# Window mixing with group normalization: group means ahead of the products, variances behind them, statistics ahead of the additions

## The chip, the cores and the metric

The kernel runs on one core of one Trainium2 chip, in float32. The metric is the device time of one execution in microseconds (us), lower is better. The engines are TensorE (PE, matrix products; PEld is its loading of weights), VectorE (DVE), ScalarE (ACT), GpSimd (POOL) and the queue that starts most transfers (SP). The change touches the first stage, the mixing of windows, and one link of the second, the projections.

## The reference

The input is x of 8 images, 256 channels, 64 by 64 pixels. Two blocks follow each other, each behind a group normalization (32 groups of 8 channels, over channels and pixels):

```
m = mean(g); s = var(g); (g - m) / sqrt(s + eps)          # per image and group
x = x + mix(gn(x), w, b)      # windows of 8x8 pixels, shifted by 4: 16 heads, each a 64x64 product over
                              # the pixels of a window, for its 16 channels, plus a bias
x = x + attention(gn(x), ...) # 1x1 projections to q, k, v, a 5x5 depthwise and a grouped 1x1 convolution,
                              # linear attention with relu, projection, batch norm
```

## The kernel before

**Stages.** `window_mixing` computes the first line and writes its result to `x1_dram`. `projections`, `convolved_heads` and `output` compute the second. A stage begins when the one before has ended on all engines. This case is about `window_mixing`, with eight images `b` in two halves `g` of rows: 16 steps `s`, even for g = 0 and odd for g = 1. The 256 channels lie on 128 partitions in two tiles (`ct`).

**One step.** The half image is normalized into `xn` (ScalarE and GpSimd, `normal_slots`), transposed by TensorE so that pixels lie on partitions (`turn`, four groups of 8 transposes, line 534), copied to `xT` by ScalarE (`fill`, line 460), multiplied with the weights (`mix`, line 559), given its bias and copied to `yT` (`add_bias`: two of eight parts by VectorE, line 683, six by ScalarE, line 468), transposed back (`turn_back`, four blocks of 8 transposes, line 571) and added to the image in place (`add_back`, VectorE, lines 698 and 702). SP then stores the half image and, when that has landed, loads the same half of the image three further on into the place.

**The order on TensorE** is written out by hand. In step s: the products of s, in four quads of heads; `turn(s + 1, 0)`, `turn(s + 1, 1)`, `turn_back(s, 0)`, `turn(s + 1, 2)`, `turn_back(s, 1)`, `turn(s + 1, 3)`, `turn_back(s, 2)`, `turn_back(s, 3)`. There are eight banks of PSUM: quad k writes banks 2k and 2k + 1, groups 0 and 2 of `turn` banks 2 and 3, groups 1 and 3 banks 0 and 1, blocks 0 and 2 of `turn_back` banks 4 and 5, blocks 1 and 3 banks 6 and 7. So block 2 waits for the addition of block 0 (`k_taken`), block 3 for that of block 1, and quad 2, the third, for all four additions of the step before. Block 0 waits for all the biases.

**The normalization of the next image** needs statistics. VectorE takes them from the image in SBUF in eight pieces a step (`moments(b + 2, g)`, line 111: `bn_stats` over 512 pixels), two images ahead. In each even step s = (b, 0) a chain for image b + 1 runs through three engines (`norm_scale`, `norm_group_sums`, `norm_std`):

- aggregate: VectorE gathers the pieces (`moments` in `norm_scale`, line 120), two instructions;
- `means`: TensorE averages the means over a group (line 161), into `stat_ps`;
- `centre`: VectorE copies the mean (127) and adds its squared distance to the variance (128 to 130), which are chained by a semaphore;
- `variances`: TensorE averages these (line 165);
- `variance`: VectorE adds eps (line 134), and increments `var`;
- root: ScalarE (line 171), behind the second `fill` of the next step;
- `scale`: VectorE makes scale and shift in six chained instructions (138 to 148); ScalarE and GpSimd wait for these with the normalization of step s + 2.

`chain_at(b, g)` says which steps have a chain: the even ones of images 0 to 6, and the last step, 15, whose chain (tiles `p_...`) is for the first image that the projections take. Both sums lie in bank 0 (`stat_ps = ps[:, 0, 0:4]`), which quad 0 fills, so TensorE takes the means behind the products and behind VectorE's bias of quad 0, the variances behind `turn(s + 1, 0)`, and `turn(s + 1, 1)`, which writes bank 0 again, waits for `var`.

**The order on VectorE** in a step: aggregate (chain step), two biases, `centre`, two pieces, `variance`, one piece, `scale`, and then four additions with a piece behind each, and the last piece. In steps without a chain it is the same without the links. Steps 12 and 14 and their odd neighbours have fewer images ahead: step 12 has no pieces; in 13 and 14 the pieces are those of the projections' first image; step 15 has none.

All engines execute their instructions in the order written, and wait for semaphores where the code says so.

Of the kernel before, what the change touches and what calls it, by code (L numbers as in the profile page):

```python
# [25 lines left out]
ALU = mybir.AluOpType  # L26
# [88 lines left out]
def norm_scale(dve, chain, b, T, mv, bst, stat_ps, sem, mean=None, normal_done=None):  # L115
# [16 lines left out]
    def variance():  # L132
        dve.wait_ge(sem["group_sum"], 2 * b + 2)
        dve.tensor_scalar(T["ve"][:, :], stat_ps[:, 2:4], GN_EPS, None, ALU.add).then_inc(sem["var"], 1)
# [22 lines left out]
def norm_group_sums(pe, b, T, mv, stat_ps, gavg, sem):  # L157

    def means():
        pe.wait_ge(sem["moments"], 2 * b + 1)  # L160
        pe.matmul(stat_ps[:, 0:2], gavg[:, :], mv[:, :, 0], start=True, stop=True).then_inc(sem["group_sum"], 1)

    def variances():
        pe.wait_ge(sem["moments"], 2 * b + 2)
        pe.matmul(stat_ps[:, 2:4], gavg[:, :], T["vc"][:, :], start=True, stop=True).then_inc(sem["group_sum"], 1)
    return means, variances
# [14 lines left out]
def make_constants(nc, ctx, two_phases, K):  # L181

    def sb(name, shape, dt=F32):
        return ctx.enter_context(nc.sbuf_tensor(name, shape, dt))
# [19 lines left out]
    K["p_mv"] = sb("pmv", [P, CT, 2])  # L204
    K["p_norm"] = norm_tiles(sb, lambda name: ctx.enter_context(nc.semaphore(name)), "p")
# [45 lines left out]
def window_mixing(nc, K, x_in, w_mix, b_mix, w_qkv, w_dw, x1_dram, taps_dram):  # L251
# [3 lines left out]
    with ExitStack() as ctx:  # L255
# [30 lines left out]
        def norm_of(b):  # L286

            return (0, K["p_norm"][0], K["p_mv"], K["p_norm"][1], None) if b == B else (b, T, mv, ns, mean)

        ps = psum("mix_ps", [P, 8, 512])  # L290
        stat_ps = ps[:, 0, 0:4]
# [206 lines left out]
        def _(pe):  # L498
            halves = (slice(0, WS * WS), slice(WS * WS, P))

            def links(b):
                image, Tn, mvn, nsn, _ = norm_of(b)
                return norm_group_sums(pe, image, Tn, mvn, stat_ps, K["gavg"], nsn)
# [35 lines left out]
            def mix(s):  # L539

                b, g = STEPS[s]
                pe.wait_ge(t_taken, N_T * (s + 1))
                for k in range(QUADS):
                    if k == 2:
                        at_least(pe, k_taken, N_K * s)
# [33 lines left out]
            for s, (b, g) in enumerate(STEPS):  # L579
                mix(s)  # L580
# [3 lines left out]
                if means:  # L584
                    pe.wait_ge(m_taken, len(BY_DVE) * s + 1)
                    means()
                if more:
                    turn(s + 1, 0)
                if variances:
                    variances()  # L590
                if more:
                    if image is not None:
                        pe.wait_ge(ns["var"], image + 1)
                    turn(s + 1, 1)
# [10 lines left out]
        def _(dve):  # L605
# [20 lines left out]
            def chain_of(b):  # L626
                image, Tn, mvn, nsn, mean_n = norm_of(b)

                def normal_done():
                    if 0 < b < B:  # L630
# [3 lines left out]
                                                            mean_n, normal_done)  # L634
# [36 lines left out]
            for g in range(GROUPS):  # L671
                for _ in moments(1, g):
                    pass
            dve.wait_ge(b_ready, 1)
# [30 lines left out]
            for s, (b, g) in enumerate(STEPS):  # L705
# [8 lines left out]
                if image is not None:  # L714
                    begin, centre, variance, scale = chain_of(image)
                    begin()
# [3 lines left out]
                if image is not None:  # L720
                    centre()
                for _ in range(2):
                    next(pieces, None)
                if image is not None:
                    variance()
                next(pieces, None)
                if image is not None:
                    scale()
                for n in range(BACKS):
                    add_back(s, n)  # L730
                    next(pieces, None)
                for _ in pieces:
                    pass
# [3 lines left out]
def projections(nc, K, x1_dram, qkv_dram, qr_dram, w_pw, bn_in, taps_dram, sorted_dram):  # L737
# [3 lines left out]
    with ExitStack() as ctx:  # L741
# [451 lines left out]
        def _(dve):  # L1193
# [64 lines left out]
            def body(i, last_body):  # L1258
                for par in range(2):
# [3 lines left out]
                    gather, centre, variance, scale = norm_scale(dve, Chain(dve, ns["chain"]), b + 1, T, mv, bst, stat_ps, ns)  # L1263
# [960 lines left out]
```

## Time and profile before

| | |
|---|---|
| median of 3 runs | 2491.38 us (2490.16 to 2492.57) |
| profiled execution | 2490.49 us, its span 2488.8 us |
| mixing stage in the profile | from 0 to 261 us |
| TensorE busy over the span | 2364.8 us, 95% |
| mean granted TensorE clock | 0.984 of full speed |

In the rows further down, a line of the timeline says when a run of like instructions started, how long it lasted, the engine, the line of the kernel and the operation, output <- input, with their number, and in brackets how long the engine idled before it and who released it. Two lines of the same engine can overlap a little, since the next instruction starts while the last one writes its end. The ends of matmuls are modelled.

### The profile page before, as it was taken

Reading aid. Unit: us, or ns where it says so; the run is one execution under the profiler, and the core shown is the slowest. Engines: PE = TensorE matmul, PEld = TensorE weight load, DVE = VectorE, ACT = ScalarE, POOL = GpSimd, SP = SyncE. Lnnn points to the kernel's source line nnn. Section 1 sums busy time; section 2 is a strip of 40 time slices with the busy share of each in tenths; the row PEclk is TensorE's granted clock in tenths of the full one; section 3 lists DMA queues with packets and bytes.
Section 4 is the critical chain, followed back from the end, with each engine's and each line's share of the span. In section 5 each row is a group of like instructions: output and inputs, shape, how many; then the busy total and the mean of one; then the engine's idle time right before and its main releaser. Section 6 shows DMA issues by size and latency. Waiting matters only on the chain. (4 is left out here: it accounts for less than half of the span.)

```text
span 2488.8 us, 66780 instructions
## 1 busy us (share of the span) xinstructions
PE 2364.8 (95%) x25485; PEld 1886.2 (76%) x25485; DVE 1992.4 (80%) x2652; ACT 1495.8 (60%) x1864; POOL 1099.0 (44%) x1477
## 2 busy tenths in 40 slices
PE   5999799999999999799999999999999889999998
PEld 5889687777787788577888888888888656666666
DVE  7887588787688786788888888888888578888775
ACT  5777576665566566566677677667767433443342
POOL 6722387787787787300000000000000068888887
PEclk9999899999999999899999999999999999999999
DMA  7874688988889889988888888888888677777774
GB/s 283 342 293 177 212 301 313 325 294 306 307 281 323 320 282 321 267 204 204 206 213 208 208 208 210 207 207 212 210 206 209 215 251 271 279 278 271 270 271 135
DMA packets 300877, 628.38 MB, mean 252 GB/s; under 512 B 50688, under 2 KB 252160, under 8 KB 291456
## 3 DMA queue, kind: packets, MB, share of 16 engines
q1 hardware_dynamic: 295616, 590.90, 77.1%
q10 hardware_dynamic: 4048, 31.11, 3.5%
q0 software_dynamic: 1008, 3.67, 0.4%
q8 instruction: 125, 2.05, 0.3%
q14 instruction: 80, 0.66, 0.1%
HBM read 327.81 MB, written 300.94 MB: 253 GB/s over the span
## 5 line engine op out<-in xcount | busy, mean ns | idle before, releaser
L1901 POOL TENSOR_TENSOR ql<-image,qh 128x1024 fp32r<-128x1024 f32 x128 | 305.3, 2410 | 971.4 <-ACT qh L1929 971.4
L1555 PE MATMUL c_ps<-dh,wh 128*128 128x512 f32 x1152 | 463.5, 402 | 17.5 <-DVE wl L1706 13.1
L1470 ACT ACTIVATE dh<-image 128x1632 fp32r<-128x1632 f32 x192 | 301.5, 1570 | 266.7 <-PE c_ps L1555 250.6
L1555 PE MATMUL c_ps<-dh,wl 128*128 128x512 f32 x1152 | 455.0, 395 | 0.0
L1555 PE MATMUL c_ps<-dl,wh 128*128 128x512 f32 x1152 | 453.6, 394 | 1.3 <-issue 1.3
L1664 DVE TENSOR_TENSOR dl<-image,dh 128x1632 fp32r<-128x1632 f32 x192 | 356.4, 1856 | 72.2 <-ACT dh L1470 72.2
L1125 PE MATMUL o_ps<-xh,wqh 128*128 128x512 f32 x768 | 320.8, 418 | 11.0 <-issue 7.6
L1125 PE MATMUL o_ps<-xl,wqh 128*128 128x512 f32 x768 | 304.6, 397 | 0.0
L1125 PE MATMUL o_ps<-xh,wql 128*128 128x512 f32 x768 | 303.4, 395 | 0.0
L1555 PEld LDWEIGHTS c_ps<-dh,wh 128*128 128x128 f32 x1152 | 217.7, 189 | 70.1 <-DVE wl L1706 13.2
L1555 PEld LDWEIGHTS c_ps<-dl,wh 128*128 128x128 f32 x1152 | 217.3, 189 | 53.4 <-issue 1.3
L1555 PEld LDWEIGHTS c_ps<-dh,wl 128*128 128x128 f32 x1152 | 217.5, 189 | 45.8
L941 POOL TENSOR_SCALAR qs<-qw 128x512 f32<-128x512 f32 x126 | 234.2, 1874 | 0.0
L1045 ACT ACTIVATE kv<-o_ps 128x512 f32<-128x512 f32 x128 | 76.9, 601 | 260.2 <-PE o_ps L1125 256.7
L2037 PE MATMUL z_ps<-qh,fh 128*128 128x512 f32 x512 | 208.5, 407 | 5.2 <-ACT qh L1929 3.6
L1950 ACT ACTIVATE zs<-z_ps,bn_shift 128x512 f32<-128x512 f32 x64 | 44.0, 687 | 281.6 <-PE z_ps L2037 281.6
L2037 PE MATMUL z_ps<-qh,fl 128*128 128x512 f32 x512 | 200.7, 392 | 0.0
L2037 PE MATMUL z_ps<-ql,fh 128*128 128x512 f32 x512 | 200.5, 392 | 0.0
L1270 DVE COPY kv<-o_ps 128x512 f32<-128x512 f32 x128 | 87.9, 687 | 123.8 <-PE o_ps L1125 123.1
L975 ACT ACTIVATE xn<-image,p_nb,p_sc 128x512 f32<-128x512 f32 (+2 forms) x160 | 175.8, 1121 | 8.4 <-PEq L255 8.4
L902 POOL TENSOR_TENSOR ptick<-ident 128x1 f32<-128x1 f32 x224 | 95.4, 426 | 184.7 <-DMA qkv_scratch<-stage 78.5
L1125 PEld LDWEIGHTS o_ps<-xh,wqh 128*128 128x128 f32 x768 | 146.4, 191 | 39.7 <-issue 14.1
(210 smaller groups left out, 5024.0 us busy)
## 6 DMA issues: line engine op xcount, KB each, us to landing
qkv_scratch<-stage SPq DMA_DIRECT2D x384, 408.0 KB, 4.0
image<-qkv_scratch SPq DMA_DIRECT2D x189, 816.0 KB, 6.3
qr_scratch<-qs SPq DMA_DIRECT2D x128, 256.0 KB, 3.0
yq_scratch<-qy SPq DMA_DIRECT2D x64, 512.0 KB, 6.7
image<-qr_scratch SPq DMA_DIRECT2D x128, 256.0 KB, 6.2
image<-yq_scratch SPq DMA_DIRECT2D x128, 256.0 KB, 5.9
ox<-x_scratch SPq DMA_DIRECT2D x8, 4096.0 KB, 14.8
out<-ox SPq DMA_DIRECT2D x7, 4096.0 KB, 12.7
```

Of the source, the lines that this page charges most:

```text
L902: pool.tensor_tensor(tick[:, k:k + 1], K["ident"][:, 0:1], K["ident"][:, 1:2], ALU.add)
L941: last = pool.tensor_scalar(qs[:, n % 2, t, :], qw[:, n % 2, t, :], 0.0, None, ALU.max)
L975: last = act.activation(dst[:, :, to:to + rows, :], src[:, :, of:of + rows, :], ACT.Identity, bias=T["nb"][:, ct:ct + 1], scale=T["sc"][:, ...
L1045: act.activation(kv[:, n % 2, 2 * u, :], o_ps[:, (2 * u) % 3, :], ACT.Copy).then_inc(kv_ready, 1)
L1125: last = pe.matmul(o_ps[:, j % 3, :], w[:, ct, P * t:P * t + P], xx[:, n % 2, ct, :], start=(k == 0), stop=(k == 5))
L1270: dve.tensor_copy(kv[:, n % 2, 2 * u + 1, :], o_ps[:, (2 * u + 1) % 3, :]).then_inc(kv_ready_v, 1)
L1470: act.activation(dh[kind][:, :], raw[kind], ACT.Copy).then_inc(hi_ready, 1)
L1555: last = pe.matmul(c_ps[:, m, :], w[hp][:, kind, part, o:o + P], cells[:, :, HALF * dy:HALF * dy + HALF * NB], start=(k == 0), stop=(k == 5))
L1664: dve.tensor_tensor(dl[kind][:, :], raw[kind], dh[kind][:, :].bitcast(F32), ALU.subtract)\
L1901: pool.tensor_tensor(two_of(ql, n, tp), two(n, tp), two_of(qh, n, tp).bitcast(F32), ALU.subtract)\
L1950: act.activation(zs[:, :], z_ps[:, 1, :], ACT.Identity, bias=bn["shift"][:, 1:2]).then_inc(z_taken, 1)
L2037: last = pe.matmul(z_ps[:, o, :], w[par][:, t, P * o:P * o + P], d, start=(m == 0), stop=(m == 3 * KT - 1))
```

## The change

In `window_mixing` the group means go to bank 2 and the group variances stay in bank 0. TensorE computes the means at the start of the step's products, ahead of quad 0, waiting only for the aggregate and for the fills; before quad 1 (the second), which writes bank 2, it waits until `centre` is done. The variances follow the products, behind VectorE's bias of quad 0, and are ahead of `turn(s + 1, 0)`.

On VectorE, the aggregate moves to the end of the step before (for image 1, ahead of step 0), behind all the pieces and ahead of the additions. `centre` comes first in the step. Behind the biases come three pieces, `variance`, one piece, `scale`, then all pieces that are left, and then the four additions without pieces between. In steps without a chain all eight pieces lie between the biases and the additions.

The chain of the projections' images gets a copy of the mean (`p_mean`) as the others have, one VectorE instruction more for each of seven images.

```diff
-def norm_scale(dve, chain, b, T, mv, bst, stat_ps, sem, mean=None, normal_done=None):
+def norm_scale(dve, chain, b, T, mv, bst, stat_ps, sem, mean=None, normal_done=None, var_ps=None):
+    var_ps = stat_ps[:, 2:4] if var_ps is None else var_ps
...
-        dve.tensor_scalar(T["ve"][:, :], stat_ps[:, 2:4], GN_EPS, None, ALU.add).then_inc(sem["var"], 1)
+        dve.tensor_scalar(T["ve"][:, :], var_ps, GN_EPS, None, ALU.add).then_inc(sem["var"], 1)
...
-        pe.matmul(stat_ps[:, 2:4], gavg[:, :], T["vc"][:, :], start=True, stop=True).then_inc(sem["group_sum"], 1)
+        pe.matmul(var_ps, gavg[:, :], T["vc"][:, :], start=True, stop=True).then_inc(sem["group_sum"], 1)
...
-        stat_ps = ps[:, 0, 0:4]
+        stat_ps, var_ps = ps[:, 2, 0:2], ps[:, 0, 2:4]
...
-            def mix(s):
+            def mix(s, means, image):
 
                 b, g = STEPS[s]
                 pe.wait_ge(t_taken, N_T * (s + 1))
+                if means:
+                    means()
                 for k in range(QUADS):
+                    if k == 1 and means:
+                        pe.wait_ge(norm_of(image)[3]["moments"], 2 * norm_of(image)[0] + 2)
                     if k == 2:
                         at_least(pe, k_taken, N_K * s)
...
             for s, (b, g) in enumerate(STEPS):
-                mix(s)
                 image = chain_at(b, g)
                 more = s + 1 < len(STEPS)
                 means, variances = links(image) if image is not None else (None, None)
-                if means:
+                mix(s, means, image)
+                if variances:
                     pe.wait_ge(m_taken, len(BY_DVE) * s + 1)
-                    means()
+                    variances()
                 if more:
                     turn(s + 1, 0)
-                if variances:
-                    variances()
-                if more:
                     if image is not None:
                         pe.wait_ge(ns["var"], image + 1)
                     turn(s + 1, 1)
...
             for g in range(GROUPS):
                 for _ in moments(1, g):
                     pass
+            chain_of(1)[0]()
             dve.wait_ge(b_ready, 1)
...
                 if image is not None:
-                    begin, centre, variance, scale = chain_of(image)
-                    begin()
+                    _, centre, variance, scale = chain_of(image)
+                    centre()
                 at_least(dve, k_full, N_K * s)
                 for k, half in BY_DVE:
                     add_bias(s, k, half)
                 if image is not None:
-                    centre()
-                for _ in range(2):
+                    for _ in range(3):
+                        next(pieces, None)
+                    variance()
                     next(pieces, None)
-                if image is not None:
-                    variance()
-                next(pieces, None)
-                if image is not None:
                     scale()
+                for _ in pieces:
+                    pass
+                if s + 1 < len(STEPS) and chain_at(*STEPS[s + 1]) is not None:
+                    chain_of(chain_at(*STEPS[s + 1]))[0]()
                 for n in range(BACKS):
                     add_back(s, n)
-                    next(pieces, None)
-                for _ in pieces:
-                    pass
...
-                    gather, centre, variance, scale = norm_scale(dve, Chain(dve, ns["chain"]), b + 1, T, mv, bst, stat_ps, ns)
+                    gather, centre, variance, scale = norm_scale(dve, Chain(dve, ns["chain"]), b + 1, T, mv, bst, stat_ps, ns,
+                                                                K["p_mean"])
```

## Rows read from the trace of the kernel before

**Rows 1.** The page's first section: busy time, share of the span, instructions.
```profile
PE 2364.8 (95%) x25485; PEld 1886.2 (76%) x25485; DVE 1992.4 (80%) x2652; ACT 1495.8 (60%) x1864; POOL 1099.0 (44%) x1477
```
**Rows 2.** Stretches from step start to step start: busy time of each engine, clock, transfers.
```profile
34.05:48.22 14.17, 12.41 (x197) 11.60 (x197) 11.96 (x30) 12.63 (x21) 8.58 (x41) 1.00 0.44 142
...
105.75:119.17 13.42, 13.42 (x258) 13.01 (x257) 10.83 (x19) 10.25 (x19) 11.97 (x64) 1.00 0.84 319
119.17:134.12 14.95, 12.74 (x197) 11.69 (x196) 12.91 (x32) 12.35 (x21) 3.99 (x9) 1.00 0.81 314
204.73:218.89 14.16, 12.76 (x197) 11.70 (x196) 10.63 (x27) 11.77 (x20) 3.40 (x8) 1.00 0.38 149
```
**Rows 3.** Waits from 34 to 262 us: us in total, times, longest us.
```profile
DVE m_r L138 <- ACT m_std L171: 12.7, 7, 2.3
...
PEld mix_ps L571 <- DVE image L702: 6.7, 8, 1.0
```
**Rows 4.** Timeline of all engines, steps 5 (odd) and 6 (even).
```profile
109.24 0.84 ACT L468 ACTIVATE yT<-mix_ps,mix_bias 128x256 f32<-128x256 f32 x2 [0.49 <-PE mix_ps L559]
...
115.00 1.22 DVE L698 TENSOR_TENSOR image<-image,mix_ps 128x1024 f32<-128x1024 f32 x1 [2.59 <-PE mix_ps L571]
...
116.75 0.94 DVE L698 TENSOR_TENSOR image<-image,mix_ps 128x768 f32<-128x768 f32 x1
...
117.33 1.91 PE L571 MATMUL mix_ps<-ident,yT 128*128 128x128 f32 x16
...
119.17 2.24 PE L559 MATMUL mix_ps<-xT,wT 64*64 64x224 f32 x64
...
121.17 0.48 DVE L702 TENSOR_TENSOR image<-image,mix_ps 128x128 f32<-128x128 f32 x2
...
121.71 2.24 PE L559 MATMUL mix_ps<-xT,wT 64*64 64x224 f32 x64 [0.30 <-DVE image L702]
122.89 0.60 DVE L120 BATCH_NORM_AGGREGATE mmv<-mbst 128x2 f32<-128x48 f32 x2
123.02 3.03 ACT L468 ACTIVATE yT<-mix_ps,mix_bias 128x256 f32<-128x256 f32 x8 [0.59 <-PE mix_ps L559]
123.40 1.22 DVE L683 TENSOR_TENSOR yT<-mix_ps,mix_bias 128x512 f32<-128x512 f32 x2
...
124.54 0.15 DVE L127 COPY mmean<-mix_ps 128x2 f32<-128x2 f32 x1
...
125.12 0.16 DVE L130 TENSOR_TENSOR m_vc<-m_sq,mmv 128x2 f32<-128x2 f32 x1
...
126.05 1.03 ACT L460 ACTIVATE xT<-mix_ps 128x1024 f32<-128x1024 f32 x1
126.40 0.14 DVE L134 TENSOR_SCALAR m_ve<-mix_ps 128x2 f32<-128x2 f32 x1
...
126.60 1.09 PE L534 MATMUL mix_ps<-ident,xnorm 128*128 128x128 f32 x8 [0.53 <-DVE m_ve L134]
...
128.65 0.20 ACT L171 ACTIVATE m_std<-m_ve 128x2 f32<-128x2 f32 x1
...
129.98 1.22 DVE L698 TENSOR_TENSOR image<-image,mix_ps 128x1024 f32<-128x1024 f32 x1
```
**Rows 5.** Timeline of all engines, end of step 6.
```profile
132.57 0.48 DVE L702 TENSOR_TENSOR image<-image,mix_ps 128x128 f32<-128x128 f32 x2
...
133.10 0.86 PEld L571 LDWEIGHTS mix_ps<-ident,yT 128*128 128x128 f32 x8 [1.00 <-DVE image L702]
```
**Rows 6.** Timeline of VectorE before and in step 0.
```profile
29.44 7.20 DVE L111 BATCH_NORM_STATS2 mbst<-image 128x6 f32<-128x512 f32 x12
36.74 0.60 DVE L120 BATCH_NORM_AGGREGATE mmv<-mbst 128x2 f32<-128x48 f32 x2
```
**Rows 7.** Timeline of TensorE in step 0, behind its products.
```profile
38.20 0.38 PE L161 MATMUL mix_ps<-mmv,gavg 128*128 128x2 f32 x2
```
**Rows 8.** Stretch in step 15, columns as in the second group.
```profile
252.70:255.00 2.30, 2.25 (x13) 2.28 (x14) 1.67 (x7) 0.01 (x1) 0.00 (x0) 0.64 0.19 78
```
**Rows 9.** Timeline of TensorE, step 15: all blocks transposed back.
```profile
252.75 5.66 PE L571 MATMUL mix_ps<-ident,yT 128*128 128x128 f32 x32 [0.48 <-ACT yT L468]
```

More of the change, by code:

```diff
@@ L154, with norm_group_sums @@
 CONST_STEPS = 7 + NPH
-def norm_group_sums(pe, b, T, mv, stat_ps, gavg, sem):
+def norm_group_sums(pe, b, T, mv, stat_ps, gavg, sem, var_ps=None):
+    var_ps = stat_ps[:, 2:4] if var_ps is None else var_ps
     def means():
@@ L204, in make_constants @@
     K["p_mv"] = sb("pmv", [P, CT, 2])
+    K["p_mean"] = sb("pmean", [P, CT])
     K["p_norm"] = norm_tiles(sb, lambda name: ctx.enter_context(nc.semaphore(name)), "p")
@@ L286, in norm_of @@
         def norm_of(b):
-            return (0, K["p_norm"][0], K["p_mv"], K["p_norm"][1], None) if b == B else (b, T, mv, ns, mean)
+            return (0, K["p_norm"][0], K["p_mv"], K["p_norm"][1], K["p_mean"]) if b == B else (b, T, mv, ns, mean)
         ps = psum("mix_ps", [P, 8, 512])
-        stat_ps = ps[:, 0, 0:4]
+        stat_ps, var_ps = ps[:, 2, 0:2], ps[:, 0, 2:4]
         w_loaded, b_loaded, b_ready = sem("w_loaded"), sem("b_loaded"), sem("b_ready")
@@ L502, in links @@
                 image, Tn, mvn, nsn, _ = norm_of(b)
-                return norm_group_sums(pe, image, Tn, mvn, stat_ps, K["gavg"], nsn)
+                return norm_group_sums(pe, image, Tn, mvn, stat_ps, K["gavg"], nsn, var_ps)
             pe.wait_ge(K["const_done"], CONST_STEPS)
@@ L633, in chain_of @@
                 start, centre, variance, scale = norm_scale(dve, Chain(dve, nsn["chain"]), image, Tn, mvn, bst, stat_ps, nsn,
-                                                            mean_n, normal_done)
+                                                            mean_n, normal_done, var_ps)
                 def begin():
```

## The prediction

> **What bounds the kernel now.** The page comes first: TensorE is busy for 95% of the span [rows 1], so what counts is what makes it wait or runs at its pace. The change touches the mixing stage, its first 261 of 2489 us, and one short link of the projections. So the next view is the one of stretches, cut where a step's products begin [rows 2]. An odd step (second half of an image; 105.75 to 119.17) lasts 13.42 us, and TensorE is busy for all 13.42: nothing can be won there and nothing late can be caught up. An even step with a normalization chain (119.17 to 134.12) lasts 14.95 us with 12.74 busy: 2.21 us idle. All that the change can win or lose in the seven chain steps 0, 2, ... 12 is here. The view of waits names the waits [rows 3]: VectorE waits 12.7 us in seven steps for the square root on ScalarE, and the transposes back wait 6.7 us for VectorE's additions (loads of weights wait with the engine).
>
> The timeline then gives the order in one even step [rows 4]; I count from its start, E = 119.17. VectorE finishes the fourth addition of the step before at E+2.48 (121.17 and 0.48), and the third quad of products, which needs its bank, starts at E+2.54. Two more pieces of statistics, the aggregate (122.89) and the biases (123.40) follow, then the chain: copy of the mean at 124.54, end of its last link at 125.12 and 0.16. The variance comes to VectorE at 126.40 at the latest, since transpose group 1 starts at 126.60 (E+7.43), having waited 0.53 for it. The root starts on ScalarE at E+9.48, behind bias additions and two fills; the first addition on VectorE starts at E+10.81, right behind the scale. The transposes back of blocks 2 and 3 wait for the first and second addition, because they reuse their banks: block 3 starts at 133.10, when the second addition ended at 133.05 [rows 5], and the odd step starts 1.02 us after that, at 134.12 (E+14.95) [rows 2].
>
> **The change, part by part.** Durations: a piece of statistics takes 0.60 us of VectorE in a row (twelve in 7.20) [rows 6]; an addition of blocks 0 and 2 takes 1.14 us until the next instruction starts (1.22 shown, overlapping at its end), one of blocks 1 and 3 1.33 (0.85 and 0.48).
>
> *1. Statistics ahead of the additions, odd step.* All eight pieces now lie before the first addition, and the next image's aggregate (a slot of 0.63: from the last piece at 36.64 to 37.3 [rows 6]) behind them. From the step's start O = 105.75: the second quad is full at O+3.49 (ScalarE starts on it then, having waited for TensorE) [rows 4], a bias 0.6, so the pieces run from O+4.1 to O+8.9, the aggregate to O+9.55. Before, the first addition started at O+9.25 (115.00), released by TensorE after 2.59 us idle. It is 0.3 us late and ends at O+10.7; block 2 is transposed back from O+11.6 (117.33), so nothing waits. The second addition starts at O+11.0 as before (116.75), since TensorE sets it, and ends at O+12.3, just as block 3 begins (O+12.4). Cost 0, with 0.07 us to spare; if it is 0.3 late, 0.3 in each of eight odd steps, 2.4 us. What is gained: additions three and four follow without a piece between, from 118.5 (block 2 transposed), so the fourth ends at 118.5 + 1.14 + 1.33 = 120.97: E+1.8, not E+2.48.
>
> *2. Means ahead of the products; centring before the second quad.* TensorE does the means at E (0.36 us, the two matmuls) and the first quad (1.04: a quarter of the 4.15 from 34.05 [rows 2] to 38.20 [rows 7]) until E+1.40. VectorE can centre only behind the fourth addition, at E+1.8; the links take 0.74 (124.54 to 125.28). So the second quad starts at E+2.60, after 1.2 us of idling, and with three quads of 1.04 the products end at E+5.7, where before they ended at E+4.6. Each later quad is 1.1 late, and with it ScalarE's biases: the last four, which began at 123.02 (E+3.85) and let the first fill start at E+6.88 [rows 4], let it start at E+7.98.
>
> *3. Variances behind the products.* 0.36 us, then transpose group 0 (0.88) without the two old waits, group 1 at E+7.0, 0.4 earlier than before. But the root's place is behind the second fill on ScalarE, and fills of about 0.96 (1.03 less their overlap, an estimate) from E+7.98 put the root at E+9.9 (before 9.48). Scale ends at E+11.25. That chain was to be early, and is 0.4 late.
>
> *4. Statistics ahead of the additions, even step.* Three pieces lie before the variance, one before the scale (it covers the wait for the root), and the last four behind the scale and before the first addition: 4 x 0.60 = 2.4 us. Before, that addition followed the scale at once. It starts at E+13.65 instead of E+10.81. TensorE, through with its block 1 and group 3 at E+11.7, now waits for it until E+13.65 + 1.22 + 0.05 = E+14.9: 3.2 us. The second addition ends at E+13.65 + 1.14 + 1.33 = E+16.1, block 3 starts at E+16.17, and 1.02 later the odd step, at E+17.19. Against 14.95 that is +2.24 us. Five steps (2, 4, 6, 8, 10): +11.2.
>
> *5. The ends.* Step 0: the aggregate now releases the products. VectorE finishes the statistics of image 1 at 36.64 and the aggregate at 37.3 [rows 6]; the products, which started at 34.05, start at 37.3 + 0.36 and end at 41.8, where the old means followed at 38.20 [rows 7]. Biases until 44.0, two fills, root at 45.9, scale until 47.2, four pieces, first addition at 49.6, step 1 at 49.6 + 1.14 + 1.33 + 1.07 = 53.1, against 48.22 [rows 2]: +4.9. Step 12 has a chain but no statistics: 11.25 + 3.54 = 14.8 against 14.16 [rows 2], +0.6. Step 14 has no chain; the old wait at the third quad goes, -0.4. Step 15: means 0.36 and a wait of some 0.55 (its first quad is longer, 1.54) delay the last biases, the root and the transposes back by 0.9; nothing overlaps the stage's end, so +0.9.
>
> *6. The projections' mean copy.* Seven times 0.19 us of VectorE (124.54 to the next link). The variance matmul sits two products later in TensorE's order, so this is hidden: 0; uncovered it is 1.3.
>
> *7. The clock.* In the last step, after a stretch with two short idle waits, the granted clock of 252.7 to 255.0 was 0.64 [rows 8], that is, it went from 2.4 to 1.2 GHz within it, and 32 transposes back took 5.66 us [rows 9], 0.177 each against 0.115 in 117.33 to 119.17. Through the chain steps it stayed at 1.00 with waits of up to 1 us between transposes. The new wait of 3.2 us lies nearer to the first. Price of one fall: the 16 transposes of blocks 2 and 3, 16 x 0.062 = 1.0 us (more if products run slow too). Six such waits give 0 to 6.0; I take half, 3.0. The Trainium skill ("TensorE: Matmul & The Clock Gate", "Why this matters for your kernels") warns that an idle gap between bursts of matmuls sends the clock back to its lower level; by it all six would fall and the sum would be 3.0 higher.
>
> **Sum.** 4.9 + 11.2 + 0.6 - 0.4 + 0.9 + 0 + 3.0 = +20.2 us. The profiled execution took 2490.49 (span 2488.8 and 1.7 around it); it would be 2510.7. The median of the runs is 0.9 above the profiled one: 2511.6.
>
> **Rivals.** *A, the compact chain wins (faster).* If the first addition of the even step is not late, TensorE's idle goes from 2.2 us to the 1.2 of part 2: 7 x 1.0 = 7 faster, 2484. It decides at one point: the addition must start by E+10.4, so that it ends before block 2 is due at E+11.7. For it speaks that VectorE idles 12.7 us in waits for the root, room for the pieces. Against it, only one of the last five pieces lies in that room; four lie behind it in VectorE's order. Chance 0.05. *B, no change.* Gains and losses cancel if the four pieces run while ScalarE's fills hold TensorE anyway, that is if block 1 and group 3 end 2.2 us later than I put them, at E+13.9, and the step before gives that back; the odd steps with no idle speak against it. 2491.4, chance 0.04. *C, as forecast, without a fall of the clock and with ScalarE not late* (the biases catch up 0.45 per step): 20.2 - 3.0 - 6 x 0.45 - 0.9 = 13.6, 2505.0; chance 0.28. *D, the clock falls at all six waits, and odd steps lose the 0.3:* 20.2 + 3.0 + 2.4 = 25.6, 2517.0; chance 0.23. By the Trainium skill's rule in part 7 the clock would do this. *The forecast:* 0.40.
>
> **How the numbers follow.** C, forecast and D together hold 0.91. The range reaches from a little under C to a little over D, 2502 to 2519, and leaves out A, B and a tail of mis-sized waits, about 0.15. A measurement of this kernel can tell about 0.2%, 5 us. Slower by over that 0.91, within it 0.04, faster 0.05.
>
> **What would show it.** In the changed profile: (1) a wait of TensorE of about 1 us inside each chain step's products, released by VectorE's last centring link, and none at the third quad; (2) no wait for the variance; (3) the root no earlier than before; (4) four pieces between scale and first addition in steps 0 to 10, and a wait of some 3 us before block 2, released by that addition; (5) even steps of about 17.2 us, odd ones of 13.4; (6) step 0 about 5 us longer, waiting for the aggregate; (7) a granted clock under 1.00 in slices of the mixing; (8) everything behind 261 us only shifted. The forecast is wrong if VectorE's first addition starts near its old place, if the odd steps grow (the margin of 0.07 us), or if a statistic meets a load of its image that has not landed, since pieces move ahead while loads follow the stores.

## The result and the profile after

The changed kernel takes 2515.14 us (median of six runs, 2506.64 to 2518.73), the kernel before 2491.59 us (2488.97 to 2492.64). The ratio is 1.01 (95% interval 1.0088 to 1.0112): about 1% slower, 23.6 us between the medians. The forecast was 2511.6 us, range 2502 to 2519. The profiled execution took 2518.73 us with a span of 2516.7, 28.2 us more than the profiled one of before. It is the slowest of the six, so what is read from its trace adds up to more than the 23.6 us.

First the page, its first section and TensorE's granted clock in 40 slices, then the same clock line of the kernel before. TensorE fell from 95% to 94% busy [rows 1]. The first slice, 63 us of the mixing, now has a clock under 0.9; before, the early slice under 0.9 was the fifth (249 to 311 us), which holds the stage's end:

```profile
PE 2373.5 (94%) x25485; PEld 1895.8 (75%) x25485; DVE 1996.8 (79%) x2660; ACT 1494.6 (59%) x1864; POOL 1099.9 (44%) x1477
...
PEclk8999999999999999899999999999999999999999
```

```profile
PEclk9999899999999999899999999999999999999999
```

Then the stretches of the changed kernel (columns as in [rows 2]), cut at step starts; the first two are the wait ahead of step 0's products and the products themselves:

```profile
34.46:37.84 3.38, 0.00 (x0) 0.03 (x1) 3.20 (x7) 2.28 (x2) 3.38 (x26) 0.62 1.06 317
37.84:44.30 6.46, 6.46 (x130) 5.74 (x130) 3.19 (x9) 2.54 (x7) 1.24 (x5) 0.67 0.43 138
...
88.84:102.63 13.79, 13.79 (x257) 13.56 (x257) 11.18 (x20) 9.11 (x17) 12.31 (x68) 0.96 0.78 298
102.63:120.84 18.21, 13.92 (x198) 13.08 (x196) 13.20 (x30) 13.54 (x22) 12.06 (x70) 0.91 0.78 297
120.84:134.17 13.33, 13.33 (x258) 13.10 (x258) 11.19 (x20) 9.12 (x17) 9.35 (x42) 1.00 0.65 246
134.17:152.28 18.11, 14.07 (x198) 13.07 (x196) 13.07 (x30) 13.53 (x22) 7.06 (x14) 0.88 0.81 315
...
229.59:244.06 14.47, 12.60 (x199) 11.52 (x197) 8.31 (x22) 12.19 (x21) 3.41 (x8) 1.00 0.37 146
244.06:257.47 13.41, 13.41 (x257) 13.02 (x256) 10.89 (x19) 10.55 (x20) 4.82 (x10) 1.00 0.40 159
257.47:269.20 11.73, 11.38 (x193) 11.10 (x193) 11.34 (x21) 10.18 (x18) 0.00 (x0) 1.00 0.47 182
```

Even steps with a chain and pieces (here steps 4 and 6) take 18.2 and 18.1 us where one took 14.95 [rows 2]. TensorE's busy time in them grew too, from 12.74 to 14.0, at a clock of 0.88 to 0.91: the same matmuls ran slower. Step 12, with a chain but no pieces, takes 14.47 against 14.16.

The waits from 34 to 286 us of the changed kernel, to set against [rows 3]:

```profile
DVE m_r L139 <- ACT m_std L173: 20.4, 7, 3.5
PEld mix_ps L579 <- DVE image L704: 20.0, 8, 3.2
...
PEld mix_ps L567 <- DVE m_vc L131: 7.3, 6, 1.3
PEld mix_ps L163 <- issue: 4.8, 1, 4.8
```

VectorE's wait for the root grew from 12.7 to 20.4 us, and the transposes back now wait 20.0 us for the first addition. The third line is the new wait for the centring ahead of the second quad.

The timeline of step 6 (all engines, in two parts) shows the order; E is 134.17, the means:

```profile
124.94 4.83 DVE L111 BATCH_NORM_STATS2 mbst<-image 128x6 f32<-128x512 f32 x8
...
130.33 1.16 DVE L704 TENSOR_TENSOR image<-image,mix_ps 128x1024 f32<-128x1024 f32 x1
...
134.17 0.28 PE L163 MATMUL mix_ps<-mmv,gavg 128*128 128x2 f32 x2
...
135.50 0.48 DVE L708 TENSOR_TENSOR image<-image,mix_ps 128x128 f32<-128x128 f32 x2
135.89 0.15 DVE L128 COPY mmean<-mix_ps 128x2 f32<-128x2 f32 x1
...
136.69 1.65 PE L567 MATMUL mix_ps<-xT,wT 64*64 64x224 f32 x40 [1.08 <-DVE m_vc L131]
```

```profile
140.39 0.14 DVE L135 TENSOR_SCALAR m_ve<-mix_ps 128x2 f32<-128x2 f32 x1
...
141.85 1.99 ACT L464 ACTIVATE xT<-mix_ps 128x1024 f32<-128x1024 f32 x2
...
143.66 0.28 ACT L173 ACTIVATE m_std<-m_ve 128x2 f32<-128x2 f32 x1
...
143.97 0.17 DVE L139 RECIPROCAL m_r<-m_std 128x2 f32<-128x2 f32 x1 [2.84 <-ACT m_std L173]
...
145.04 2.46 DVE L111 BATCH_NORM_STATS2 mbst<-image 128x6 f32<-128x512 f32 x4
...
147.42 2.07 DVE L704 TENSOR_TENSOR image<-image,mix_ps 128x1024 f32<-128x1024 f32 x2
148.68 3.27 PEld L579 LDWEIGHTS mix_ps<-ident,yT 128*128 128x128 f32 x16 [3.07 <-DVE image L704]
148.68 3.67 PE L579 MATMUL mix_ps<-ident,yT 128*128 128x128 f32 x16 [2.84 <-DVE image L704]
```

The variance is ready 3.3 us ahead of the root, which stands behind two fills. VectorE idles 2.84 us for it, and only then does four pieces, 2.4 us, with TensorE waiting. The 16 transposes of blocks 2 and 3 then take 3.67 us; at the full clock, with VectorE's pause of 0.17 between the blocks, they take 2.35 (shown below, in the kernel kept busy and in the repeat).

### The profile page after: what moved, and what is told of

Its sections match the earlier page's. It is cut to its first block and busy times, and to the rows that moved or that the text cites. A ratio compares the mean times of both kernels' runs of the same rounds, so it can differ in the third digit from the quotient of the medians.

```text
span 2516.7 us, 66782 instructions
## 1 busy us (share of the span) xinstructions
PE 2373.5 (94%) x25485; PEld 1895.8 (75%) x25485; DVE 1996.8 (79%) x2660; ACT 1494.6 (59%) x1864; POOL 1099.9 (44%) x1477
## 3 DMA queue, kind: packets, MB, share of 16 engines
q0 software_dynamic: 1008, 3.67, 0.4%
## 5 line engine op out<-in xcount | busy, mean ns | idle before, releaser
L1560 PE MATMUL c_ps<-dh,wh 128*128 128x512 f32 x1152 | 463.4, 402 | 16.5 <-DVE wl L1711 13.4
L1560 PEld LDWEIGHTS c_ps<-dh,wh 128*128 128x128 f32 x1152 | 217.5, 189 | 68.9 <-DVE wl L1711 13.5
L945 POOL TENSOR_SCALAR qs<-qw 128x512 f32<-128x512 f32 x126 | 239.9, 1920 | 0.0
## 6 DMA issues: line engine op xcount, KB each, us to landing
out<-ox SPq DMA_DIRECT2D x7, 4096.0 KB, 12.7
```

Source lines behind the costliest of these rows:

```text
L945: last = pool.tensor_scalar(qs[:, n % 2, t, :], qw[:, n % 2, t, :], 0.0, None, ALU.max)
L1560: last = pe.matmul(c_ps[:, m, :], w[hp][:, kind, part, o:o + P], cells[:, :, HALF * dy:HALF * dy + HALF * NB], start=(k == 0), stop=(k == 5))
```

## The experiments

All were timed beside the kernel before, in three sessions on three chips. Its medians there were 2489.04, 2488.88 and 2489.36 us, against 2491.59 above, so the kernels are compared by their ratio to the kernel before; 0.001 is 2.5 us. "Start of the projections" is the first product of the next stage in the profiled execution: 267.18 us before, 292.00 after, and 288.29 in a repeat of the changed kernel. That repeat comes further down; its ratio, 1.0086 (1.0073 to 1.0099), is lower than the first 1.01, and the variants are held against both.

**The last pieces put back between the additions**, chain steps only.

```diff
                     scale()
-                for _ in pieces:
-                    pass
+                if image is None:
+                    for _ in pieces:
+                        pass
...
                     add_back(s, n)
+                    next(pieces, None)
```

> The changed kernel, but in steps with a chain the last four pieces of statistics go back between the additions. Theory (late additions): the first addition again starts right behind the scale, at about E+11.3, TensorE's wait of 3 us before block 2 shrinks to under 1 us, the clock no longer falls there, even steps take about 15.5 us in place of 17.7 to 18.2 and odd ones 13.4. Time about 2497 us (2515.1 less 6 x 2.5 and 2.7 for the odd steps). Rival (centring before the second quad makes the loss): the wait of 1.1 us there and the late biases stay, so at most 5 us come back, 2510 or more.

Measured: 2498.52 us, ratio 1.0041 (1.0028 to 1.0055); start of the projections 272.56. The products of odd steps begin at 111.26 and 139.62, so two steps take 28.4 us, as before (28.4 from 105.75 to 134.12 [rows 2]). More than half of the loss is gone, though the wait of 1.1 us ahead of the second quad is still there, six times. The rival falls.

**The last pieces put into the wait for the root.**

```diff
                     variance()
-                    next(pieces, None)
+                    for _ in range(5):
+                        next(pieces, None)
                     scale()
```

> The changed kernel, but the last four pieces run before the scale, in the time in which VectorE waits for the root on ScalarE; the additions stay without pieces between. Theory: the four pieces cost nothing there (a wait of 2.8 us, 2.4 us of pieces), the first addition starts at E+11.3 and the even step takes about 14.8 us, a little under the 14.95 of the kernel before. Time about 2494 us, the rest above before being step 0 (5 us or more). Rival (the centring wait is the loss): 2510 or more. Rival (clock alone): the clock no longer falls, so this one and the one with the pieces between the additions would be equal.

Measured: 2495.48 us, ratio 1.0024 (1.0014 to 1.0034). Its timeline in step 6 (all engines):

```profile
129.28 3.06 DVE L111 BATCH_NORM_STATS2 mbst<-image 128x6 f32<-128x512 f32 x5
...
132.18 0.27 ACT L173 ACTIVATE m_std<-m_ve 128x2 f32<-128x2 f32 x1
...
133.58 2.09 DVE L704 TENSOR_TENSOR image<-image,mix_ps 128x1024 f32<-128x1024 f32 x2
...
134.86 1.09 PE L579 MATMUL mix_ps<-ident,yT 128*128 128x128 f32 x8 [0.50 <-DVE image L704]
```

The five pieces end as the root starts, and cost nothing. The addition starts 2.4 us earlier after the scale, the wait ahead of block 2 is 0.50 us, and the step from 122.69 to 137.14 takes 14.45 us: less than the 14.95 of before, and 3.66 less than the 18.11 of the changed kernel. These four pieces, with the falls of the clock behind the wait they make, are the main cause: some 15 to 19 us of the whole (1.01 or, in the repeat, 1.0086, against 1.0024).

**Step 0 in the old order**: means behind the products, centring behind the biases; all else as changed.

```diff
-                mix(s, means, image)
+                mix(s, means if s > 0 else None, image)
+                if means and s == 0:
+                    pe.wait_ge(m_taken, len(BY_DVE))
+                    means()
...
-                    centre()
+                    if s > 0:
+                        centre()
...
                     add_bias(s, k, half)
                 if image is not None:
+                    if s == 0:
+                        centre()
```

> The changed kernel, but in step 0 the means come behind the products and the centring behind the biases, as before. Theory: step 0 (22.3 us from the last fill to step 1 in the changed kernel, 14.2 before) starts its products at once instead of waiting 3.4 us for the aggregate, and they run at the higher clock (4.2 instead of 6.0 us); the late additions of step 0 stay. About 17 us, 5 us saved: 2510 us. Rival (the products hide behind something else): under 2 us saved, 2513 or more.

Measured: 2507.73 us, ratio 1.007 (1.0056 to 1.0083). TensorE's timeline of step 0 in this kernel, and then in the changed one:

```profile
34.17 4.21 PE L567 MATMUL mix_ps<-xT,wT 64*64 64x224 f32 x128 [1.21 <-ACT xT L464]
...
52.03 6.24 PE L567 MATMUL mix_ps<-xT,wT 64*64 64x224 f32 x192
```

```profile
37.84 0.56 PE L163 MATMUL mix_ps<-mmv,gavg 128*128 128x2 f32 x2 [4.62 <-DVE mmv L121]
38.33 6.04 PE L567 MATMUL mix_ps<-xT,wT 64*64 64x224 f32 x128
...
53.14 3.68 PE L579 MATMUL mix_ps<-ident,yT 128*128 128x128 f32 x16 [2.83 <-DVE image L704]
56.74 7.33 PE L567 MATMUL mix_ps<-xT,wT 64*64 64x224 f32 x192
```

From the last fill to step 1 it is 17.9 us instead of 22.3: the wait for the aggregate goes, and the 128 matmuls take 4.21 us instead of 6.04. By ratio 4 to 7 us come back. Against the repeat alone the times do not settle it (the two intervals overlap, and the projections start at 287.99 against 288.29, with a fall of the clock behind all five waits that are left); the 4.4 us are read from the timeline.

**One part alone on the kernel before**: in chain steps the pieces that are left behind the scale go ahead of the additions (five here, four in the changed kernel); means, variances and centring stay where they were.

```diff
                 if image is not None:
                     scale()
+                    for _ in pieces:
+                        pass
```

> The kernel before, with one part of the change alone: in steps with a chain the five pieces left behind the scale run before the additions. Theory: the first addition starts 3.0 us later (E+13.8), the even steps take about 17.3 instead of 14.95 us, six of them, +14.4; the clock falls at these waits and adds about 1.3 each: 2491.5 + 22 = 2513 us. Without falls of the clock 2506. Rival (pieces are hidden, the loss comes from the centring and the means): unchanged, 2492.

Measured: 2504.31 us, ratio 1.0067 (1.0054 to 1.0081), 17 us slower by ratio, nearer to the value without falls of the clock. In the profile three of the six waits, all of 3.0 to 3.1 us, have a fall behind them. Even steps without a fall take 17.29 us (130.53 to 147.82), as worked out; with one, 18.6. This part alone makes the larger share of the whole loss.

**TensorE kept busy in the wait.** 26 transposes of a constant into a free bank, ahead of block 2 in steps 0 to 10.

```diff
+                if g == 0 and b + 2 < B:
+                    pe.wait_ge(t_taken, N_T * (s + 1) + 3)
+                    for _ in range(26):
+                        pe.transpose(ps[:, 2, 0:P], K["ident"][:, :], K["ident"][:, :])
                 turn_back(s, 2)
```

> The changed kernel, with 26 transposes of a constant into free bank 2 put into TensorE's wait before block 2 in steps 0 to 10 (about 2.9 of the 3.2 us; they compute nothing that is used). Theory (the clock falls because TensorE idles there): the granted clock stays at 1.00 in blocks 2 and 3 and the products of the odd steps, even steps take 17.2 us instead of 17.7 to 18.2, odd ones 13.4 instead of 13.3 to 14.4, and the runs scatter less. About 7 us back, 2508 us. Rival (the falls cost nothing, since VectorE sets the pace there): 2515 or, with the work added, more.

Measured: 2507.5 us, ratio 1.007 (1.0057 to 1.0083). Its stretches from step 4 on, and TensorE's timeline at the end of step 4 (L609 is the added work):

```profile
98.50:115.42 16.92, 15.38 (x224) 14.30 (x222) 12.92 (x30) 13.50 (x22) 11.34 (x64) 1.00 0.89 349
...
128.70:145.61 16.91, 15.24 (x225) 14.43 (x223) 12.93 (x30) 13.66 (x22) 5.74 (x11) 1.00 0.82 320
```

```profile
110.03 3.00 PE L609 MATMUL mix_ps<-ident 128*128 128x128 f32 x26
113.14 1.09 PE L579 MATMUL mix_ps<-ident,yT 128*128 128x128 f32 x8
114.40 1.09 PE L579 MATMUL mix_ps<-ident,yT 128*128 128x128 f32 x8 [0.17 <-DVE image L712]
115.42 4.83 PE L567 MATMUL mix_ps<-xT,wT 64*64 64x224 f32 x150
```

With more work the kernel is faster: the projections start at 281.65 us, against 292.00 and 288.29 in the two profiles of the changed kernel. The clock stays at 1.00 behind all six waits, even steps take 16.8 to 17.0 us and all odd ones 13.3. VectorE still sets the addition, so this is the lateness without the clock: 1.9 us a step (84.3 us for the five steps 2 to 10, against 75.0 before). The clock's falls cost the rest, 4 to 7 us by ratio; the interval lies clear of the first 1.01 and overlaps that of the repeat. Whether the runs scatter less, as expected, is not shown: they spread over 7.6 us, the two samples of the changed kernel over 12 and 2.8.

**The projections without the copy of the mean.**

```diff
-        chain.base, chain.n = (NORM_CHAIN + (mean is not None)) * b, 0
+        chain.base, chain.n = (NORM_CHAIN + (mean is not None)) * b + extra, 0
...
-                    gather, centre, variance, scale = norm_scale(..., stat_ps, ns, K["p_mean"])
+                    gather, centre, variance, scale = norm_scale(..., stat_ps, ns, extra=1)
```

> The changed kernel without the copy of the mean in the projections (the scale reads the mean from PSUM again). Theory: hidden behind two products, no difference to the changed kernel, 2515 us within its scatter. Rival: seven times 0.19 and what queues behind it, 1 to 3 us less; the changed kernel's part behind the mixing is 3.1 us longer than before in the profiled execution.

Measured: 2510.94 us, ratio 1.0084 (1.0071 to 1.0097), against 1.0086 for the changed kernel in the repeat. In the profile the part from the start of the projections to the end is 2224.0 us (2509.2 less 285.19), against 2224.7 with the copy, and 2218.5 with the copy in the repeat. No effect can be seen.

**The changed kernel once more**, for the clock.

> The changed kernel once more, on the same chip as the others of this call. Theory: the clock falls in most of the six waits before block 2, but not in the same ones for equal lengths of time; ratio to before 1.009 to 1.011, and blocks 2 and 3 together take between 1.9 (no fall) and 3.7 us (whole at the lower clock) per step. Rival (the falls are a feature of one execution): no falls, 2505.

Measured: 2510.39 us (2509.18 to 2511.94), ratio 1.0086 (1.0073 to 1.0099). TensorE's timeline, three of the waits:

```profile
84.54 1.09 PE L579 MATMUL mix_ps<-ident,yT 128*128 128x128 f32 x8 [2.84 <-DVE image L704]
85.80 1.09 PE L579 MATMUL mix_ps<-ident,yT 128*128 128x128 f32 x8 [0.17 <-DVE image L708]
114.79 3.30 PE L579 MATMUL mix_ps<-ident,yT 128*128 128x128 f32 x16 [2.95 <-DVE image L704]
...
207.15 3.67 PE L579 MATMUL mix_ps<-ident,yT 128*128 128x128 f32 x16 [2.83 <-DVE image L704]
```

After the same wait (2.84 and 2.83 us) the 16 transposes run in 2.35 us from the first start, with VectorE's pause of 0.17, or in 3.67. Four of six waits were followed by a fall here, six of six in the first profile, three of six in the kernel without the copy. Over the five profiles with this wait left as it is (these three, step 0 in the old order, and the one part alone), 20 of the 27 waits of 2.83 to 3.08 us before block 2 had a fall behind them. What chooses stays open. Two things of the expectation were wrong: the lower bound of 1.9 without a fall, as the pause belongs to it, and the ratio, which came out at 1.0086, just under 1.009 to 1.011.

**The root ahead of the fills on ScalarE**, all else as changed.

```diff
+                    if image is not None and image < B:
+                        norm_std(act, image, T, ns)
                     for f in range(FILLS):
                         fill(s + 1, f)
-                        if f == 1 and image is not None and image < B:
-                            norm_std(act, image, T, ns)
```

> The changed kernel with one line moved: on ScalarE the root comes before the first fill instead of behind the second. Theory: the root starts at about E+8.0 instead of E+9.5, scale and the four pieces end at about E+11.8, the wait of TensorE before block 2 shrinks from 3 to about 1.2 us, the clock does not fall in most steps; even steps about 15.4 us. Time 2497 us. Rival (ScalarE's fills are what TensorE needs, a root ahead of them costs as much): 2512 or more.

Measured: 2495.79 us, ratio 1.0023 (1.0012 to 1.0034). Two steps take 28.3 us (111.46 to 139.75) against 31.4 in the changed kernel (120.84 to 152.28). The wait before block 2 is 0.9 to 1.05 us, and no fall is behind it. With this line moved, the four pieces behind the scale cost little, because the scale is early; it is the second way to cure the same wait.

**The centring in the step before.** Means ahead of block 2 of that step, centring between its second and third addition, step 0 in the old order, and the pieces in the wait for the root.

```diff
+                if after is not None:
+                    pe.wait_ge(t_taken, N_T * (s + 1) + 3)
+                    links(after)[0]()
                 turn_back(s, 2)
...
                 for n in range(BACKS):
                     add_back(s, n)
+                    if n == 1 and after is not None:
+                        centre()
```

> The kernel with the last pieces in the wait for the root, plus means and centring in the step before (step 0 in the old order), the root in its old place. It prices the wait before the second quad. Theory: the wait of 1.1 us before the second quad goes, the fills start 1.1 us earlier, and even steps take about 13.5 us instead of 14.45: with step 0, about 10 us less than that kernel, 2486. Rival (the centring wait is hidden behind ScalarE): even steps stay at 14.4, only step 0 gains, 2491.

Measured: 2486.09 us, ratio 0.9991 (0.9981 to 1.0001). No wait ahead of the second quad is left, but the even steps are of two kinds. VectorE and TensorE in step 6 and in step 10 (starts 118.96 and 175.99):

```profile
123.83 1.88 DVE L111 BATCH_NORM_STATS2 mbst<-image 128x6 f32<-128x512 f32 x3 [1.83 <-DMA image<-in_x]
...
125.83 1.09 PE L538 MATMUL mix_ps<-ident,xnorm 128*128 128x128 f32 x8 [1.40 <-DVE m_ve L135]
```

```profile
179.12 1.88 DVE L111 BATCH_NORM_STATS2 mbst<-image 128x6 f32<-128x512 f32 x3
...
186.63 1.09 PE L577 MATMUL mix_ps<-ident,yT 128*128 128x128 f32 x8 [0.50 <-DVE image L715]
```

In step 10 the pieces find their image loaded, and the step takes 12.92 us, 1.5 less than the 14.45 with the centring wait. Of these, 0.3 us only moved to the odd step with the means (13.59 us against 13.32), and 1.26 us a pair of steps are left (26.51, from 175.99 to 202.50, against 27.77): the wait of 1.08 us was on the path with its whole length. In step 6 VectorE waits 1.83 us for the load of the image, the variance stands behind these pieces, transpose group 1 behind the variance, and the step takes 14.34 us. So the expectation of 13.5 was right for neither; a new bound, the transfers, takes the gain back.

**Root ahead of the fills and pieces spread**: three, variance, two, scale, one, two additions, one, two additions, one; step 0 in the old order.

> The changed kernel with step 0 in the old order, the root before the fills on ScalarE, and the pieces spread: three, the variance, two, the scale, one, two additions, one, two additions, one. Theory: the root starts at E+8.0, the first addition at about E+10.0 and nothing waits for it; only the wait before the second quad (1.1 us) is left. Even steps 13.7 to 14.1 us, step 0 about 14, odd ones 13.4: 2485 us, 5 under the kernel before. Rival (the biases on ScalarE, late by 1.1 us, set the pace anyway): even steps 14.4 as with the pieces in the wait for the root, 2490.

Measured: 2487.87 us, ratio 0.999 (0.9978 to 1.0002). Step 5 and 6 together take 26.7 us (104.68 to 131.41), 1.6 less than before, with the second quad still waiting. Other pairs take 26.7 to 28.7: here too VectorE waits for loads, 5.5 us in three places. The ratio's interval includes 1, so a gain in the whole time is not shown.

**Both together**, in two forms: three pieces ahead of the variance and three behind it, then two and four.

> The kernel built from the theory. Root before the fills, step 0 in the old order; for all other chains the means are taken by TensorE before block 2 of the step before and centred by VectorE between that step's second and third addition, so that no quad waits for them; pieces: three, the variance, three, the scale, one behind the first addition, one behind the last. Theory: no wait of TensorE over 0.5 us is left in an even step, which takes 12.6 to 13.0 us instead of 14.95: seven steps, about 14 to 16 us under the kernel before, 2475 us. Rival (VectorE, with 12.3 us of work in such a step, becomes the bound and delays the third quad or the odd step's second addition): 13.5 us or more a step, 2482 or more.

> The kernel with the root before the fills and the centring in the step before, with two pieces instead of three ahead of the variance and four instead of three behind it. Theory: the wait of transpose group 1 for the variance (0.2 to 0.9 us in five steps of that kernel, 4.4 in total) goes; even steps 12.5 us instead of 12.55 to 13.3. Two to four us less than that kernel, 2483. Rival (it comes back as a wait for the first addition, since the pieces only move): no difference.

Measured: 2486.57 us, ratio 0.9992 (0.9982 to 1.0001), and 2485.99 us, ratio 0.9985 (0.9976 to 0.9994). The second is the only kernel here whose interval lies below the one before. The start of the projections is at 260.07 and 260.47, 7 us earlier than before; the expectation was 14 to 16. The view of waits of the second one, 40 to 290 us, one line, which the kernel before does not have at all:

```profile
DVE mbst L111 <- DMA image<-in_x: 12.5, 8, 3.0
```

A store and the load behind it take turns on the SP queue, and each has to land. In the first of the two kernels a store started at 132.75 and the load behind it at 142.55, 9.8 us later; before, the like stores took 7.1 to 7.6 us (108.27 to 115.70), in the changed kernel already up to 8.7 (122.33 to 130.98). A faster step moves the same bytes in less time, the pieces come sooner after the load, and VectorE waits for it. No version with the loads reordered was tried.

The loads are not the whole of it. TensorE stops inside the products of steps 3 and 7, for nothing that the profile shows. TensorE's timeline of the second kernel:

```profile
82.72 1.72 PE L565 MATMUL mix_ps<-xT,wT 64*64 64x112 f32 x39 [1.78 <-issue]
```

Steps 3 and 7 take 16.11 and 14.94 us there, steps 1, 5, 9 and 11 take 13.6, so 3.9 us go in these two; in the kernel before they took 13.97 and 13.85 against 13.4. The transfer engines' share is 1.01 and 1.02 in these two stretches of products (76.09 to 84.40, 132.80 to 140.00) and 0.59 in the same products of step 1; that the transfers cause the stops is not shown.

Of the 7 us, the medians show 2 and 4 at the end, and the profiled rest of the kernel varies by more than the difference (below), so where it goes stays open.

## Why the prediction was right, point by point

The time lay in the range, and the mechanism was the one described. That it came within 4 us is in part luck: the even steps were put too dear, step 0 and the clock too cheap. A table of the terms, from the profiled execution (steps from start to start):

| term | forecast | measured |
|---|---|---|
| odd step, late first addition | 0 | 0: addition at O+9.5 (forecast O+9.55), step 13.3 at full clock |
| even steps 2 to 10, without the clock | +11.2 (2.24 each) | +9.3 (1.9 each, from the kernel kept busy) |
| step 0 | +4.9 | +8.1 (22.3 against 14.2) |
| step 12 | +0.6 | +0.3 |
| step 14 | -0.4 | -0.7 |
| step 15 to the projections | +0.9 | +0.3 |
| clock, all waits | +3.0 | +7.1 net in steps 1 to 11 (16.3 in all, less 9.3); the falls themselves 8.7 |
| behind the mixing | 0 | +3.1 (profiled execution) |

*Part 1* held to 0.1 us: eight pieces from O+4.1, no wait of TensorE.

*Part 2* held: the second quad waited 1.08 to 1.22 us, released by the centring link, and the products ended at E+5.7. Taken away, it gave back 1.26 us a pair of steps where nothing else held VectorE (26.51 against 27.77).

*Part 3* held in its sense: the variance was 3.3 us ahead of the root, and the root no earlier (E+9.5; forecast 9.9). The prediction put all that follows 0.4 us too late (the first addition at E+13.65, measured E+13.25), and that is the difference between 2.24 and 1.9.

*Part 4*, the four pieces behind the scale, is the main cause, shown both ways: taken out of that place the kernel regains 15 to 19 us, put there alone (with a fifth) the kernel before loses 17.

*Part 5*, step 0: the wait for the aggregate was foreseen, 3.4 us. The step that was mis-sized is that the clock was left out here: TensorE had idled 4.62 us, the granted clock was 0.62 in that stretch and 0.67 in the products, and 128 matmuls took 6.04 us instead of 4.2. That is 1.8 us, and the late addition of the same step met a fall too (3.68 for the two blocks, 1.3 too long): together the 3.2 by which the step was missed.

*Part 7*, the clock: its falls were foreseen at half the waits and 1.0 us each. They came at six of six, four of six and three of six. The price of one was mis-sized. In the first profile, from the start of block 2 to the next products, the transposes took 3.16 to 3.60 us instead of 2.28, which is 6.8 us over the six; and the fall runs on into the next products, which the prediction had only in brackets: they took up to 7.34 us instead of 6.24, 3.2 us over the steps. Together 10.0 us, 1.7 a fall; 8.7 of it lies in steps 1 to 11. The kernel kept busy reaches the projections 10.4 us earlier than this profile, which agrees. The price of 1.0 came from [rows 9], where 0.177 us a transpose mixes both levels; wholly at the lower one it is 0.225 (3.60 for 16). The net in steps 1 to 11 (56.74 to 229.59 is 172.85 us; before, 48.22 to 204.73, 156.5) is smaller, 7.1, because the odd steps gained 0.1 each and steps 3 and 7 of the kernel before were 1.0 us longer than its other odd ones. The Trainium skill ("TensorE: Matmul & The Clock Gate", "Why this matters for your kernels") warns that an idle gap between bursts of matmuls brings the lower clock; by that rule the clock term would have been 3.0 larger, 6.0. The first profile agrees with the number of falls, six of six, though they cost 10.0 us; in the repeat, waits of 2.84 and 2.83 us had no fall, so the trace does not bear out that every such gap brings it.

*Part 6* and what lies behind the mixing: the copy is hidden. The first profiled execution lost 3.1 us there all the same (2224.7 against 2221.6); the repeat of the same kernel gained 3.1 (2218.5). The same stretch varied from 2217.3 to 2228.9 us over the profiles of the variants, with the projections unchanged, so this is not laid to the change.

*Rivals.* The compact chain (faster) needed the first addition by E+10.4; it came at E+13.3. The kernel with the root ahead of the fills and the pieces spread meets it (its addition starts at E+9.6), and two of its steps take 26.7 us against 28.4. So its condition was right for the steps, and the change missed it by four pieces and two fills; its gain of 7 us did not arrive in the whole time (ratio 0.999). What even that rival did not see is that the loads come due, and the stops of TensorE in steps 3 and 7. B (no change) falls: TensorE was through with block 1 and group 3 at E+11.7, as forecast, and waited 2.84 us. Of C and D each holds a part: the falls came at all six waits in the first profile, as D has it, but the odd steps lost nothing.

## What to carry to other kernels

Work that is there to fill a wait belongs ahead of the instruction that waits, and a chain should not be moved forward before one has found the link that can't overtake on another engine's queue (here the root, behind two fills): four pieces behind a wait of 2.8 us cost their length six times, in that wait nothing. A wait of some 3 us on TensorE can have a second price, the clock behind it, which a sum of durations at full clock leaves out. And before steps are made shorter, look at the margin of the loads that follow the stores.

## What was not expected of the hardware

- Adding 26 idle transposes in each of six steps made the kernel faster (1.007 against 1.0086 to 1.01): the granted clock behind them stayed at 1.00, where it was 0.50 to 0.63 over blocks 2 and 3 in the first profile.
- Equal waits, unequal clock: behind waits of 2.84 and 2.83 us in one execution, 16 block transposes in 2.35 us and in 3.67, the second for whole blocks at the lower of the two levels (a granted clock near 0.5, 1.2 GHz, where 1.00 is 2.4 GHz). Whether this makes the whole time scatter more is not shown: the first six runs of the changed kernel spread over 12 us (2506.64 to 2518.73), five of the repeat over 2.8, and 29 of the kernel before over 10.2 (2483.77 to 2493.96).
- The loads were close to coming due: the kernel before has no wait of VectorE for them from 40 us on, the kernels with the shortest steps have 5.5 to 12.5 us in all, and from a store to the load behind it took up to 9.8 us instead of 7.4.
- TensorE can stop in the middle of a run of products that waits for nothing in the profile: 1.78 us in step 3 of the fastest kernel, at a transfer share of 1.01.
